# Head-group tiles and convolutions shared among three engines in a two-block attention kernel

## The reference: what is computed

```
# block 0                                   # block 1
qkv = gn(x) @ w_qkv.T + b                   qkv = gn(x) @ qkv_w + b   (plus a rank-16 LoRA term on q and v)
q, k, v = LN(dwconv3x3(q)), LN(dwconv3x3(k)), LN(dwconv3x3(v))
attn = softmax(q @ k.T * scale + rel_h + rel_w)   # 256 x 256 for each head, both blocks
o = attn @ v + q                            o = attn @ v
x = x + o @ w_proj.T + b                    x = x + o @ proj_w + b
```

## Time and profile before

| | us |
|---|---|
| median of 3 runs (lowest, highest) | 109.63 (109.55, 111.31) |
| profiled execution, its own time | 108.68 |
| its span, first to last instruction | 106.7 |
| PE busy | 97.1 |
| DVE busy | 62.7 |
| ACT busy | 51.3 |
| POOL busy | 31.4 |

### The profile page before, as it was taken

How to read it: one execution, slowest core, us unless ns; L and a number is a source line. 1 busy time by engine, 2 the same in 40 slices (tenths; PEclk the granted TensorE clock), 3 DMA queues, 4 the chain that set the end, 5 groups by cost and what they waited for, 6 DMA issues and landing times.

```text
span 106.7 us, 2097 instructions
## 1 busy us (share of the span) xinstructions
PE 97.1 (91%) x822; PEld 70.8 (66%) x825; DVE 62.7 (59%) x134; ACT 51.3 (48%) x115; POOL 31.4 (29%) x46
## 2 busy tenths in 40 slices
PE   5799999999959999999999999899989999999780
PEld 2155787578848986777856563797759879857440
DVE  3469995587999667834650135464796493560130
ACT  4011904663534981837815624254246668715820
POOL 8947600599999999000000000000000000000000
PEclk9995579999999999999999999999999999999999
DMA  2999980000000000000000000000000000000002
GB/s 59 308 307 292 237 79 0 3 0 6 0 0 0 9 0 0 0 0 6 0 0 0 0 6 0 0 0 0 0 0 6 0 0 6 0 0 0 0 0 74
DMA packets 2826, 3.73 MB, mean 35 GB/s; under 512 B 305, under 2 KB 2242, under 8 KB 2818
## 3 DMA queue, kind: packets, MB, share of 16 engines
q0 software_dynamic: 784, 0.79, 6.7%
q1 hardware_dynamic: 1282, 1.41, 4.8%
q10 hardware_dynamic: 752, 1.42, 4.5%
HBM read 3.42 MB, written 0.20 MB: 34 GB/s over the span
## 4 chain that ended last, share of the span: by engine, by line
PE 75%; DVE 10%; ACT 7%; DMA 3%; issue 2%
PE bank L917 9%; PE bank L760 8%; PE bank L853 6%; PE bank L850 6%; PE bank L749 6%; PE bank L892 5%; PE bank L905 5%; PE bank L866 5%; PE bank L893 4%; PE bank L831 3%; ACT pt L386 3%; DVE taps_m L622 3%; DMA x<-x_t 3%; PE bank L734 3%; PE bank L832 2%
## 5 line engine op out<-in xcount | busy, mean ns | idle before, releaser
L575 DVE TENSOR_REDUCE mx<-bank 128x2 fp32r<-128x512 f32 x24 | 15.0, 682 | 3.2 <-PE bank L866 3.2
L386 ACT ACTIVATE pt<-bank 128x512 f32<-128x512 f32 x24 | 13.0, 594 | 3.6 <-PE bank L893 3.4
L892 PE MATMUL bank<-qs,ks 128*128 128x256 f32 x48 | 13.3, 310 | 0.8 <-ACT pt L386 0.7
L570 DVE SCALAR_TENSOR_TENSOR qs<-qs,vec,bank 64x512 fp32r<-64x512 f32 x12 | 8.8, 737 | 6.9 <-ACT qs L376 6.8
L893 PE MATMUL bank<-mt,nhot_r 128*128 128x256 f32 x48 | 12.0, 280 | 0.0
L892 PEld LDWEIGHTS bank<-qs,ks 128*128 128x128 f32 x48 | 9.0, 187 | 2.8 <-ACT pt L386 1.8
L760 PE MATMUL bank<-pad,taps_m 128*128 128x256 f32 x36 | 10.5, 445 | 0.2 <-DVE taps_m L622 0.2
L734 PE MATMUL bank<-warm 128*128 128x512 bf16 x28 | 9.0, 443 | 1.5 <-POOL warm L279 1.3
L324 POOL TENSOR_SCALAR tap_p<-pad,vec 64x256 f32<-64x256 f32 (+1 forms) x11 | 10.3, 937 | 0.0
L749 PE MATMUL bank<-xn,w 96*128 96x256 f32 (+1 forms) x40 | 9.6, 428 | 0.6 <-DVE xn L549 0.6
L376 ACT ACTIVATE qs<-bank 64x512 fp32r<-64x512 f32 x12 | 7.1, 590 | 6.2 <-PE bank L853 6.2
(11 more groups left out here) (103 smaller groups left out, 166.7 us busy)
## 6 DMA issues: line engine op xcount, KB each, us to landing
ks<-hots POOLq DMA_DIRECT2D x1, 768.0 KB, 7.8
wp<-w_proj ACTq DMA_DIRECT2D x1, 576.0 KB, 8.1
w<-w_qkv SPq DMA_DIRECT2D x1, 432.0 KB, 8.8
w<-w_qkv SPq DMA_DIRECT2D x1, 288.0 KB, 4.8
cst<-consts ACTq DMA_DIRECT2D x1, 256.0 KB, 4.8
nhot<-neg_hot ACTq DMA_DIRECT2D x1, 256.0 KB, 5.7
x<-x_t SPq DMA_DIRECT2D x1, 192.0 KB, 3.3
wpq<-w_proj_q ACTq DMA_DIRECT2D x1, 192.0 KB, 8.9
```

The costliest lines, as they stand in the source:

```text
L386: act.activation(pt[:, h, :, :], key_banks[h % 2][:, :].rearrange("p (k n) -> p k n", k=QT), ACT.Exp).then_inc(exped[b], 1)
L575: dve.tensor_reduce(mx[:, h, :], ring_bank(h // 4, 4 + h % 4)[:, :].rearrange("p (q n) -> p q n", q=QT), AXX, ALU.max).then_inc(maxed[b], 1)
L892: pe.matmul(dst, ks[:, h, k * 128:(k + 1) * 128], qs[:, h, :], start=True, stop=False)
```

## The change

- The tiles of q and k become **T0, T1, T2**: rows 0 to 63 hold q and rows 64 to 127 k of heads 0 to 3, 4 to 7 and 8 to 11. The columns of the weights are permuted on the host. One tile then feeds a whole stage, so q and k of stage 0 are picked one after the other (no `late_k`).
- The taps are shared: T0 has 3 on TensorE and 6 on VectorE; T1 has 5 and 4; C has 5 on VectorE and 4 on GpSimd; T2 has 6 and 3; E has 9 on GpSimd. TensorE's taps go into the PSUM bank into which `centre_tile` then adds the products of the other engines' sums.
- Five tap matrices in place of 18: q and k have the same tap columns in T0 and T1, so T1 uses the three of T0 (VectorE) and two more that ScalarE makes.
- `normalise` multiplies by the gain and the reciprocal root in one instruction; the bias is added by ScalarE in `high` and by VectorE in `low`, and by `residual` (ScalarE, three of 64 rows) for the residual q. Only C and E still have a separate `full` (`value`).
- The stage slots are filled anew; `lora_first` moves behind T0's variance, both `lora_second` into stage 2, `q_project(0)` behind stage 2, `add_w` and the clearing of `mt` behind or between GpSimd's taps.
- The input is loaded in two halves, on SP's and on ScalarE's DMA queue; the `hots` table comes from a full copy in DRAM; the warm-up operand is 128 columns wide, read four times, with 8 and 5 warm-ups in place of 7 and 4.

```diff
+PE_TAPS = {T0: range(0, 3), T1: range(0, 5), C: (), T2: (), E: ()}
+DVE_TAPS = {T0: range(3, 9), T1: range(5, 9), C: range(0, 5), T2: range(0, 6)}
+POOL_TAPS = {C: range(5, 9), T2: range(6, 9), E: range(0, 9)}
 # loads
-            sp.dma_start(xs[0][0:HALF], x_t.rearrange("(t p) n -> p t n", p=HALF)).then_inc(d_x, 16)
+            sp.dma_start(xs[0][0:HALF, 0], x_t[0:HALF]).then_inc(d_x[0], 16)
+            act.dma_start(xs[0][0:HALF, 1], x_t[HALF:]).then_inc(d_x[1], 16)
 # normalise (VectorE) and high (ScalarE)
-                dve.tensor_tensor(nrm[0:r, t, :], cen_e[:] if t == E else cen_ps[t][0:r], rstd[0:r, t, :], ALU.mult).then_inc(scaled, 1)
-                dve.wait_ge(scaled, n)
-                dve.tensor_scalar(full[0:r, t, :], nrm[0:r, t, :], vec[0:r, LNG0 + t:LNG0 + t + 1],
-                                  vec[0:r, LNB0 + t:LNB0 + t + 1], ALU.mult, ALU.add).then_inc(full_set, 1)
+                dve.scalar_tensor_tensor(out=nrm[0:r, t, :], in0=cen_e[:] if t == E else cen_ps[t][0:r],
+                                         scalar=vec[0:r, LNG0 + t:LNG0 + t + 1], in1=rstd[0:r, t, :],
+                                         op0=ALU.mult, op1=ALU.mult).then_inc(scaled, 1)
-                act.activation(hi[:, place3[t], :], full[:, t, :], ACT.Copy).then_inc(hi_set[0], 1)
+                act.activation(hi[:, t, :], nrm[:, t, :], ACT.Identity,
+                               bias=vec[:, LNB0 + t:LNB0 + t + 1]).then_inc(hi_set[0], 1)
 # VectorE, block 0
-            for k in range(TAPS):
-                taps(B, k, k + 1)
-                tap_matrices(1, k, k + 1)
-            normalise(A)
+            taps(T1, 0, 4)
+            normalise(T0)
 ...
-            stage(0, 0, {0: k_in, 2: lambda: taps(D, 2, 4), 3: lambda: taps(D, 4, D_SPLIT)})
-            normalise(C)
-            stage(0, 1, {1: lambda: normalise(D), 2: low_d_and_v})
-            stage(0, 2, {1: lambda: add_lora(1), 2: lambda: normalise(E)})
+            stage(0, 0, {1: lambda: taps(C, 1, 3), 4: t1_norm, 2: t1_low, 3: masks})   # t1_low: low(T1), taps(C, 3, 5)
+            taps(T2, 0, 3)
+            c_norm()
+            stage(0, 1, {0: lambda: taps(T2, 3, 5), 1: lambda: taps(T2, 5, 6), 2: lambda: normalise(T2), 3: t2_in})
+            add_lora(0)
+            stage(0, 2, {1: lambda: add_lora(1), 2: lambda: (normalise(E), value(E))})
 # ScalarE, block 0
-            stage(0, 0, {0: lambda: high(B), 1: lambda: tile_stats(C), 2: lambda: tile_rstd(C), 3: lambda: tile_stats(D)})
-            stage(0, 1, {0: lambda: tile_rstd(D), 1: lambda: high(D)})
+            stage(0, 0, {0: lambda: tile_stats(T1), 4: k_stats, 1: after_first, 3: c_in})
+            stage(0, 1, {0: lambda: residual(T1), 1: lambda: tile_stats(T2), 2: lambda: tile_rstd(T2), 3: lambda: high(T2)})
 # TensorE, block 0
-            project(0, 0, A, w0)
-            project(0, 1, B, w0)
-            convolve(A, 0, 0, TAPS)
-            project(0, 2, C, w0)
-            variance(A)
-            project(0, 3, D, w0)
-            centre_tile(B)
-            project(0, 4, E, w0)
-            variance(B)
-            convolve(C, 1, 0, 2)
+            project(0, T0)
+            project(0, C)
+            project(0, T1)
+            convolve(T0, 0, 3)
+            centre_tile(T0)
+            project(0, T2, (0,))
+            variance(T0)
+            project(0, T2, (1,))
+            lora_first()
+            convolve(T1, 0, 4)
 ...
-            stage(0, 0, {0: lambda: convolve(C, 1, 2, 5), 4: lambda: convolve(C, 1, 5, TAPS)})
-            variance(C)
-            centre_tile(D)
-            warm_up(1, bank[5])
-            stage(0, 1, {0: lambda: variance(D), 1: lambda: warm_up(1, bank[5]), 3: lambda: turn(C), 4: lambda: lora_second(0)})
-            stage(0, 2, {1: lambda: lora_second(1), 2: q_and_e, 3: x_and_e, 5: lambda: turn(E)})
+            stage(0, 0, {1: t1_centre, 2: lambda: variance(T1), 4: project_e})   # t1_centre: convolve(T1, 4, 5), centre_tile(T1)
+            centre_tile(C)
+            stage(0, 1, {0: lambda: variance(C), 6: lambda: centre_tile(T2), 3: lambda: variance(T2), 4: lambda: turn(C)})
+            stage(0, 2, {0: lambda: lora_second(0), 1: lambda: lora_second(1), 2: q_and_e, 3: x_and_e, 5: lambda: turn(E)})
+            q_project(0)
             last_stage(0)
```

More of the change, by code:

```diff
@@ L402, in stage @@
                 move(b, s, 0)
-                if not late_k(b, s):
-                    move(b, s, 1)
+                move(b, s, 1)
                 if g >= 1:
@@ L498, in high1 @@
             def high1(t):
[L500 to L508, removed]
+                act.wait_ge(projected[1], t + 1)
+                act.activation(hi[:, t, :], qkv1_ps[t], ACT.Identity,
+                               bias=vec[:, BQKV1 + t:BQKV1 + t + 1]).then_inc(hi_set[1], 1)
+            high1(T0)
+            high1(T1)
+            stage(1, 0, {1: lambda: high1(T2)})
             stage(1, 1)
@@ L753, in convolve, with project @@
-            def convolve(t, v, first, last):
-                r = ROWS[t]
-                if first == 0:
-                    pe.wait_ge(qtaps_set if v == 0 else vtaps_set, TAPS)
-                    pe.wait_ge(padded, order0.index(t) + 1)
-                for k in range(first, last):
-                    mm = pe.matmul(cen_ps[t][0:r, :], taps_m[:, v, k, 0:r],
-                                   pad[:, t, k // 3:k // 3 + SIDE, k % 3:k % 3 + SIDE],
-                                   start=(k == 0), stop=(k == TAPS - 1))
-                    if k == TAPS - 1:
-                        mm.then_inc(centred, 1)
+            def project(b, t, halves=(0, 1)):
+                r, col = ROWS[t], FIRST[t]
+                for k in halves:
+                    if t == T0:
+                        pe.wait_ge(xn_set[b], k + 1)
+                    mm = pe.matmul((qkv_ps, qkv1_ps)[b][t][0:r, :], (w0, w1)[b][:, k, col:col + r], xn[:, k, :],
+                                   start=(k == 0), stop=(k == 1))
+                    if k == 1:
+                        mm.then_inc(projected[b], 1)
@@ new lines, in convolve @@
+            def convolve(t, first, last):
+                for k in PE_TAPS[t][first:last]:
+                    if k == 0:
+                        pe.wait_ge(padded, n_padded[t])
+                    if t == T0:
+                        pe.wait_ge(taps_d, k + 1)
+                    if t == T1 and k == PE_TAPS[T0].stop:
+                        pe.wait_ge(taps_a, MATRICES - PE_TAPS[T0].stop)
+                    pe.matmul(cen_ps[t], taps_m[:, k, :], pad[:, t, k // 3:k // 3 + SIDE, k % 3:k % 3 + SIDE],
+                              start=(k == 0), stop=False, skip_group_check=True)
@@ new lines, in centre_tile @@
+            def centre_tile(t):
+                r = ROWS[t]
+                parts = []
+                if t in DVE_TAPS:
+                    pe.wait_ge(conv_step[t], len(DVE_TAPS[t]))
+                    parts.append(conv[0:r, conv_slot[t], :])
+                if t in POOL_TAPS:
+                    pe.wait_ge(p_sum, pool_sums(t))
+                    parts.append(conv_p[0:r, pool_order.index(t), :])
+                if t == T2:
+                    pe.wait_ge(lora_c, 1)
+                if t == E:
+                    pe.wait_ge(s_logged[0], 1)
+                for n, part in enumerate(parts):
+                    mm = pe.matmul(cen_ps[t][0:r], centre[0:r, 0:r], part, start=(n == 0 and not PE_TAPS[t]),
+                                   stop=(n == len(parts) - 1), skip_group_check=True)
+                mm.then_inc(centred, 1)
```

390 lines of the change are left out of this document (202 added, 188 removed).

## The result

The changed kernel takes 115.10 us (median of 4 runs, 114.89 to 116.18) against 109.59: a ratio of 1.0529, 95% interval 1.0446 to 1.0611. It is slower by 5%. Medians here are of all executions; ratios compare only those within 1.5% of their kernel's fastest. 109.2 was forecast, in a range that ended at 111.7.

What follows compares the result with a forecast made beforehand. TensorE was taken as the bound, half-clocked from 8.00 to 14.80, with VectorE binding near stage 0's end. Stage gains ran to about 0; 108.68 - 0.4 = 108.3, and the median 0.95 above gave 109.2 us, range 106.6 to 111.7.

Steps and rivals of the forecast that it cites:

- The bound, and block 1 at nothing: TensorE bounds most stretches, VectorE stage 0's end; block 1 costed at nothing, under 0.2 us if D's cover were gone.
- Step 1, the input: Start of block 0: input in two halves on two queues, taken as 0.3 us earlier.
- Steps 2 and 3, stage 0: Block 0: T0 centred 2.0 us earlier, near 15.0; rel units near 20.6; scores 4.2 earlier, near 24.7.
- my case with 10%: Start: the clock never falls, T0 centred near 12.2, 2.8 us less, 106.4; chance 10%.
- My sign of being wrong: At the start: the prediction is wrong if the clock's low stretch is not 8 to 15.
- Steps 4 to 6, VectorE eats the lead: Stages 0 and 1: maxima 3.3 us earlier, rel units 2.0, `weigh` 0.7; 3.5 us eaten by VectorE's taps.
- Contended taps: VectorE taps beside GpSimd: 0.56 us each, not 0.6; ten taps give 0.4 us back.
- Step 7, stage 2: Stage 2: moved `lora_second` and `q_project(0)` return on TensorE; the gain is gone, +0.1 us, running total about 0.
- The sum: Whole kernel: 108.68 - 0.4 = 108.3 us for an execution like the profiled one.
- the clock falls in stage 1 (10%): Stage 1: an idle gap before the rel units drops TensorE to 1.2 GHz, +2.6 us, 111.8; chance 10%.

Runs made afterwards that it cites:

- e13: Changed kernel plus ten fp32 matmuls (T2's first five tap products) into an unread bank in stage 1's gap, VectorE keeping its taps: 111.80 us.
- e9: Changed kernel with each rel unit's second loop (horizontal position term) left out: 105.88 us.
- e10: Kernel before the change with each rel unit's second loop (horizontal position term) left out: 105.77 us.
- e4: Changed kernel with seven warm-ups added in stage 1's gap, after the k pick: 115.95 us.
- e6: Kernel before the change without six of tile C's nine taps: five runs at 109.47 to 109.74 us, five at 112.19 to 112.54.
- e14: e15's kernel with `q_project(0)` behind stage 2 and `residual(T2)` late, as in the change: 112.49 us.
- e15: Changed kernel with five of T2's VectorE taps on TensorE in stage 1's gap, and e3's `q_project(0)` edit: 106.98 us.
- e3: Changed kernel with `q_project(0)` back between stage 2's rel units and `residual(T2)` ahead of it: 115.33 us.
- e5: Changed kernel with one warm-up on zeros in the middle of each rel unit: 123.21 us.
- e11: Changed kernel with two fp32r matmuls on real data in the middle of each rel unit: 123.98 us.
- e1: Kernel before the change with only the changed start (input in halves, narrow warm-up operand, 8 and 5 warm-ups): 110.16 us, ratio 1.0047.
- e12: e15's kernel with two of T2's five tap products moved between stage 0's rel units (so missing from T2): 111.60 us.

## Why the prediction was wrong

*The bound, and block 1 at nothing:* failed. Block 1's matmuls are the same, but one of its stretches fell to 1.2 GHz, 1.5 us.

*Step 1, the input:* right. `xn` starts 0.2 earlier (6.81 before the change, 6.62 after), TensorE's first projection too (7.40 and 7.17), where I took 0.3.

*Steps 2 and 3, stage 0:* I had T0 centred at 15.0, the rel units at 20.6 and the scores at 24.7. They came at 12.6, 18.62 and 23.07. The difference is the clock at the start, my case with 10%; the case's own figure was 12.2. It was one of two starts that this kernel has, and a third of the profiled executions had the other, so the profile's early figures are partly luck. My sign of being wrong, a low stretch that is not at 8 to 15, came true, and it did not make the kernel faster.

*Steps 4 to 6, VectorE eats the lead:* right. The lead of 5.8 us at the scores is 3.9 at stage 1's rel units. TensorE is idle for 0.98 us there in e13, in which no clock falls, until VectorE's move of q ends at 30.71 (the row says "issue", so the wait is read from VectorE's timeline), and `weigh` at 39.04 leaves 2.5, after another 1.09 us of waiting for VectorE's copy of v (`va`). Contended taps lay 0.55 to 0.6 apart, where 0.56 was taken; GpSimd stayed hidden.

*Step 7, stage 2:* half right. `lora_second` and `q_project` came back in front of `last_stage` as computed. I missed that `residual(T2)` stands on ScalarE behind stage 2's `o_copy`, which waits for `weigh`; the moved `q_project` waits 0.99 us for it. I had counted the instructions of the moved step and not whom it now waits for.

*The sum:* with no fall, e13's execution took 108.19 where the sum for an undisturbed execution was 108.3. Its errors offset each other, so this is partly luck: the fast start left 2.5 us at stage 1's `weigh`, where the sum had 1.1 (0.7, and 0.4 for the taps), and the missed wait took 0.99 back. By block 1 nothing is left: its first rel units start at 71.44 in e13 and at 71.30 before. So even without a fall the changed kernel gains next to nothing over one with 6.8 us at half clock (spans of 106.4 and 106.7). e9 and e10 say the same to about 1 us.

*The step that failed is the term for the clock.* The sum had none: it took TensorE's clock behind the start as unchanged, and the one rival for it, "the clock falls in stage 1 (10%)", had a single fall. Its place and its price were right (+2.6; measured 2.7). But three falls cost time, 2.7, 2.8 and 1.5 us, 7.0 together in the profiled execution, and the mean clocks of 0.910 to 0.925 put 17 to 20 us at half speed in all four. I made the length of the idle gap the rival's condition, and the earlier trace rows had shown a gap without a fall. e4 filled the gap and the fall stayed.

What makes the falls likely is shown in part only. e6, e13, and e14 against e15 fit dense matmul work around the rel units moving the chance of a fall; e3, e5 and e11 put work there and did not get the clock back. The change took such work away in three places: C's tap products around stage 0's units; in stage 1 the centring, the picks and single warm-ups that stood right ahead of the units (from 31.69 to 34.76), where now the units follow an idle stretch directly; and `q_project` from between stage 2's units. My sum gave none of these a price in clock. That the two single warm-ups were left out of stage 1 was not tested by itself.

The Trainium skill, TensorE: Matmul & The Clock Gate, Part 1, ties the clock to how busy TensorE has been. Busy time as the profile counts it did not hold the clock here: at 22.1 and 49.4 it fell with TensorE busy for all of the 3 us before.

*Open:* why 1.6 us of warm-ups on zeros in the gap did not do what 2.15 us of fp32 products did (amount, data or format), why the fillers inside the units failed, why the same move of `q_project` counts in e14 and e15 and not in e3, and what decides whether a given execution falls. e9 still fell twice with two thirds of the rel units' small matmuls gone, so their number alone does not decide it either.

## What to carry to other kernels

Moving dense matmuls away from TensorE's thin stretches can cost more than it saves: price each stretch at both clock levels. A kernel's runs then spread with the clock, so compare times beside each run's mean clock before explaining a difference by order, and read the level at the start from durations, since the mean can miss it. When a step is moved, look up whom its operands' producers now stand behind.

## What the runs showed that I had not expected

- The clock fell with TensorE busy for 3.58 of 3.58 us (18.62 to 22.20), 48 of the 54 matmuls being those of rel units.
- The granted clock reads 1.00 at the start even where TensorE runs at half speed: e1's five warm-ups took 2.29 us under a mean clock of 0.999, the same five 1.24 in the changed kernel's profile.
- Every fall measured lasted 3.4, 6.8 or 10.2 us, and nothing in between (changed kernel: 3.41, 6.83, 6.83, 3.41; e3 and e12: 10.24).
- A filler of 0.215 us between the loops of a rel unit lengthened the unit by 0.38 us (stage 0's first unit in e5).
